# A fused two-layer transformer kernel: the first FFN's scales spread by the matrix engine, its weights issued later, all engine orders replaced

## The chip, the cores and the metric

The kernel runs on one NeuronCore of a Trainium2 chip. Its engines work side by side, each on its own queue: TensorE (PE, matrix products; PEld is its weight load), VectorE (DVE), ScalarE (ACT), GpSimd (POOL) and SyncE (SP), which here only issues DMAs. Results of PE land in PSUM, eight banks of 128 partitions by 512 fp32. The metric is the device time of one execution in microseconds; the median of three runs of the kernel before is 828.52 us (827.58 to 831.6).

## The reference

Sixteen sequences ("chunks", 0 to 15) of 256 tokens by 128 features go through two layers, each an attention and an FFN, with a residual sum and a layer norm after each of the four stages. All in fp32.

```python
x = layernorm(x + attn0(x))   # low-rank q, k; 16 heads of 8; causal
x = layernorm(x + ffn0(x))    # ternary weights with scales, below
x = layernorm(x + attn1(x))   # 16 heads of 8; not causal
x = layernorm(x + ffn1(x))    # top-1 expert: base weights plus a LoRA of rank 4

def tlin(x, w, s):            # w: 512x128, 512x512 or 128x512; s: one scale per output
    return jnp.einsum('bsi,oi->bso', x, w) * s
h = silu(tlin(x, w1, s1)) * tlin(x, w2, s2)
h = gelu(tlin(h, h1, hs1))
h = gelu(tlin(h, h2, hs2))
ffn0 = tlin(h, w3, s3)
```

## The kernel before

Each stage of a chunk is cut into steps, and one letter stands for each kind of step (table `KIND`). For every engine a string in `SEQUENCE` gives the order of its steps over all chunks and stages, and `walk` calls them in that order; `BANK_TABLE` says which PSUM bank each PE step writes. So the order is written out by hand, and an engine that waits for a semaphore holds up all that stands behind it. Stages of different chunks are interleaved: while chunk 5 is in its first FFN, chunk 6 is in its first attention, and so on.

The steps that matter here:

- `qk` projects queries and keys (PE, L955); ACT and DVE split them into two parts (L604/L608 and L719), SP writes them to a DRAM scratch ("parks" them, L471) and reads them back spread over the partitions ("fetches" qrow and krow, L480 and L484). `pass1` (PE, L988; the causal mask by L995) makes the scores from them, and DVE takes their row maxima (L745).
- `maxima` turns the maxima (PE, L1019); DVE splits them (L778, L780); SP writes them to `mrow` (L492). `pass2` makes the scores again (L1044), turned, and subtracts the maxima through `mrow` (L1052, L1059); ACT takes the exponential (L622), POOL masks (L565), `values` is the product with v (L1077), `project` the output product (L1089).
- Chunk 0 goes without scratch: its queries and keys lie in `hid` and in `prob`; `early` and `maxima` turn its maxima by L1005.
- The first FFN: `gated` (L1110), `hidden` (L1128, four steps of 8 products), `down` (L1185). Its ternary weights are multiplied by their scales once, at the start, on DVE: step `scale` with k = 0 (w12, L699 and L700), 1 and 2 (wh, 128x2048 each, L711), 3 (w3, L704).
- Step `late` is ACT issuing weight loads: k = 0 the scales, read from DRAM 128 times so that all partitions hold them, and w12; k = 1 both halves of wh (1 MB each) and w3; k = 2 the ten loads for layer 1.
- SP's `load` brings the next chunk's input, both ways round, once PE has used the buffer's last content.

## Time and profile before

| | us |
|---|---|
| median of 3 runs | 828.52 |
| the profiled execution | 828.5 |
| its span (first to last instruction) | 826.8 |
| PE busy | 792.4 |
| DVE busy | 619.0 |
| ACT busy | 412.1 |
| POOL busy | 186.3 |

1.7 us of the profiled execution lie around the span. PE is busy for 96% of it, so what counts is the time in which PE idles or runs at a lower clock, and the amount of work given to it. "PEclk" is the clock granted to PE as a share of full speed; a window at 0.50 is one at 1.2 instead of 2.4 GHz. A matmul record can be half of a product: L1128 has 8 products in a step and 16 records. "Idle before" is the time for which the engine stood still before a group, with the instruction whose end released it.

### The profile page before, as it was taken

The numbers are of one execution on the slowest core, as the hardware profiler recorded it, in microseconds if no ns is written. First come the engines' busy times: TensorE is split into PE (matmuls) and PEld (weight loads), VectorE is DVE, ScalarE is ACT, GpSimd is POOL, SyncE is SP. The second block draws the span as 40 slices with busy tenths as digits, with TensorE's granted clock in tenths as the row PEclk, the third lists the DMA queues.
The fourth block names the chain that finished last, engine by engine and source line by source line (L and its number), as shares of the span: only waits on it lengthen the run. The fifth ranks groups of instructions, "written<-read, shape, count | busy, mean of one in ns | idle before, by whom it ended". The sixth has DMA issues, their size and how long they took to land.

```text
span 826.8 us, 21566 instructions
## 1 busy us (share of the span) xinstructions
PE 792.4 (96%) x8626; PEld 610.8 (74%) x8626; DVE 619.0 (75%) x1749; ACT 412.1 (50%) x829; POOL 186.3 (23%) x397
## 2 busy tenths in 40 slices
PE   8879999999999999999999999999999999999796
PEld 6557777777778687887768777776878777786575
DVE  3666696886888697978779776788968776476775
ACT  1223517364744638374463646355393636636372
POOL 4221303031301313140222312130132303101022
PEclk9769999999999999999999999999999999999799
DMA  4652221304130314004050220304131110101200
GB/s 144 197 199 78 66 105 49 123 28 143 35 135 17 105 60 144 33 29 142 17 163 19 98 81 29 128 5 141 57 103 54 33 55 22 59 29 59 90 10 27
DMA packets 42572, 64.31 MB, mean 78 GB/s; under 512 B 5128, under 2 KB 33128, under 8 KB 42088
## 3 DMA queue, kind: packets, MB, share of 16 engines
q1 hardware_dynamic: 40696, 57.93, 21.5%
q10 hardware_dynamic: 1776, 5.00, 1.9%
q8 instruction: 69, 1.13, 0.6%
q14 instruction: 31, 0.25, 0.1%
HBM read 43.54 MB, written 18.35 MB: 75 GB/s over the span
## 4 chain that ended last, share of the span: by engine, by line
PE 79%; DMA 8%; DVE 5%; ACT 3%; SPq 2%; issue 2%; POOL 1%; POOLq 0%; DVEq 0%; ACTq 0%
PE banks L1128 26%; PE banks L1077 10%; PE banks L1044 6%; PE banks L988 6%; PE banks L1185 6%; PE banks L1110 6%; DMA krow<-scratch 5%; PE banks L955 3%; PE banks L1157 3%; DMA scratch<-split 2%; PE banks L1089 2%; PE banks L964 2%; ACT prob L622 2%; PE banks L1059 2%; PE banks L1052 2%
## 5 line engine op out<-in xcount | busy, mean ns | idle before, releaser
L745 DVE TENSOR_REDUCE top<-banks 128x3 f32<-128x384 f32 (+1 forms) x512 | 286.6, 613 | 50.5 <-PE banks L988 24.9
L622 ACT ACTIVATE prob<-banks 128x384 f32<-128x384 f32 (+1 forms) x512 | 242.5, 559 | 82.3 <-PE banks L1052 30.3
L636 ACT ACTIVATE hid<-banks 128x512 f32<-128x512 f32 x64 | 38.2, 597 | 211.8 <-PE banks L1128 211.6
L1077 PE MATMUL banks<-prob,v 128*32 128x256 f32 (+1 forms) x2048 | 117.9, 364 | 2.0 <-DVE low L875 1.2
L1128 PE MATMUL banks<-glu,wh 128*128 128x256 f32 x512 | 118.2, 384 | 0.1
L1128 PE MATMUL banks<-hid,wh 128*128 128x256 f32 x512 | 117.4, 382 | 0.2
L558 POOL TENSOR_TENSOR ln_rstd<-ln_var,minus_half 128x2 f32<-128x2 f32 x64 | 44.7, 702 | 320.7 <-DVE ln_var L824 320.4
L1128 PEld LDWEIGHTS banks<-glu,wh 128*128 128x128 f32 x512 | 94.8, 190 | 14.9 <-issue 1.1
L1128 PEld LDWEIGHTS banks<-hid,wh 128*128 128x128 f32 x512 | 94.8, 190 | 13.9 <-DVE top L745 1.2
L1077 PEld LDWEIGHTS banks<-prob,v 128*32 128x32 f32 x2048 | 58.9, 111 | 41.3 <-issue 10.0
L563 POOL TENSOR_TENSOR pool_carrier<-minus_half 128x1 f32<-128x1 f32 x128 | 25.3, 197 | 278.7 <-ACT prob L622 278.4
L988 PE MATMUL banks<-krow,qrow 32*128 32x256 f32 (+1 forms) x992 | 73.1, 337 | 10.7 <-DMA krow<-scratch 9.2
L565 POOL TENSOR_SCALAR_AFFINE_SELECT prob<-prob 128x512 f32<-128x512 f32 x128 | 83.2, 650 | 0.0
L988 PEld LDWEIGHTS banks<-krow,qrow 32*128 32x128 f32 x992 | 45.3, 189 | 44.9 <-issue 18.8
L1044 PE MATMUL banks<-qrow,krow 32*128 32x256 f32 x992 | 67.8, 325 | 1.4 <-issue 0.7
L1044 PEld LDWEIGHTS banks<-qrow,krow 32*128 32x128 f32 x992 | 43.6, 188 | 34.1 <-issue 21.3
L1110 PE MATMUL banks<-xt,w 128*128 128x256 f32 x256 | 63.9, 395 | 0.6 <-DVE top L745 0.5
L1110 PEld LDWEIGHTS banks<-xt,w 128*128 128x128 f32 x256 | 47.5, 194 | 9.4 <-issue 2.2
L786 DVE STREAM_TRANSPOSE osum<-banks 128x256 f32<-128x256 f32 x64 | 28.2, 442 | 31.8 <-PE banks L1077 31.7
L553 POOL TENSOR_TENSOR resid<-x,rows 128x256 f32<-128x256 f32 x48 | 35.2, 738 | 35.4 <-DVE ln_sum L811 35.3
L834 DVE TENSOR_SCALAR x<-ln_sum,ln_stat,ln_rstd 128x128 f32<-128x128 f32 x96 | 35.9, 418 | 8.6 <-POOL ln_rstd L558 8.6
L650 ACT ACTIVATE inter<-banks,cols 128x256 f32<-128x256 f32 x64 | 25.2, 488 | 25.9 <-PE banks L1165 25.8
(113 smaller groups left out, 1024.9 us busy)
## 6 DMA issues: line engine op xcount, KB each, us to landing
scratch<-split SPq DMA_DIRECT2D x124, 128.0 KB, 2.2
qrow<-scratch SPq DMA_DIRECT2D x31, 512.0 KB, 3.8
krow<-scratch SPq DMA_DIRECT2D x62, 256.0 KB, 4.3
xt<-in_xt SPq DMA_DIRECT2D x16, 128.0 KB, 2.2
wh<-in_wh ACTq DMA_DIRECT2D x2, 1024.0 KB, 6.3
out<-xout SPq DMA_DIRECT2D x16, 128.0 KB, 2.1
x<-in_x SPq DMA_DIRECT2D x15, 128.0 KB, 2.3
prob<-in_qk_a SPq DMA_DIRECT2D x2, 512.0 KB, 5.4
```

The costliest lines, as they stand in the source:

```text
L558: nc.gpsimd.tensor_tensor(ln_rstd[s][:], ln_var[s][:], minus_half[:], ALU.pow).then_inc(rstd[s], 1)
L565: nc.gpsimd.affine_select(out=diag, in_=diag, compare_op=ALU.is_ge, fill=0.0, base=0, pattern=[[0, 2], [0, QB], [1, P]], channel_multiplie ...
L622: nc.scalar.activation(prob[s][:, j % 2, g, 0:wide], banks[:, b, 0:wide], ACT.Exp, scale=1.0 / float(np.sqrt(np.float32(HD))) if s == A0 e ...
L636: nc.scalar.activation(hid[layer][:, 2 * m:2 * m + 2, :].rearrange("p m t -> p (m t)"), banks[:, g, :], ACT.Gelu).then_inc(gelued, 1)
L745: nc.vector.tensor_reduce(out=top[s][:, :, h], in_=banks[:, b, 0:blocks * wide].rearrange("p (q k) -> p q k", q=blocks), axis=AX, op=ALU.m ...
L834: done = nc.vector.tensor_scalar(x[into[s]][n % AHEAD][:, t, :], ln_sum[s][:, t, :], ln_stat[s][:, t, 0:1], ln_rstd[s][:, t:t + 1], ALU.su ...
L988: done = nc.tensor.matmul(banks[:, bs[g], start:start + wide], of_tile(queries, g, j, bass.ts(qb, P)), of_tile(keys, g, j, slice(0, wide)) ...
L1044: done = nc.tensor.matmul(banks[:, bs[g], kb * SEQ:(kb + 1) * SEQ - q0], of_tile(keys, g, j, bass.ts(kb, P)), of_tile(queries, g, j, slice ...
L1077: done = nc.tensor.matmul(banks[32 * i:32 * i + 32, g, q0:SEQ], v[s][:, kb, GROUP * j + i, :], prob[s][:, j % 2, i, kb * SEQ:(kb + 1) * SE ...
L1110: done = nc.tensor.matmul(banks[:, g, i * TOK:(i + 1) * TOK], w12[:, side, (2 * m + i) * P:(2 * m + i + 1) * P], xt[F0][n % AHEAD][:], sta ...
L1128: done = nc.tensor.matmul(banks[:, g, i * TOK:(i + 1) * TOK], wh[:, layer, k, (2 * m + i) * P:(2 * m + i + 1) * P], (glu, hid[0])[layer][: ...
L1185: done = nc.tensor.matmul(banks[:, g, t * D:(t + 1) * D], src[:, k, t * P:(t + 1) * P], w[:, k, :], start=k == 0, stop=k == HB - 1)
```

## The change

The scales are loaded into one partition (8 KB instead of 1 MB). PE multiplies a row of ones with them, one 512-wide fp32 product for each of the four sets, into PSUM, and DVE reads the scales for w12 and wh from there. So `scale` is now also a PE step (two products for k = 0, one each for k = 1 and 2) and takes banks. `late` has four parts instead of three: wh's first half, then wh's second half and w3, are issued separately. All five strings of `SEQUENCE` and the whole bank table are new; DVE's k = 0 to 2 no longer wait for the weights1 load. All other work is as before in kind and number.

```diff
-BARE = ('load', 'late', 'scale', 'keys', 'resid', 'fetch', 'norm', 'store', 'outputs')
+BARE = ('load', 'late', 'keys', 'resid', 'fetch', 'norm', 'store', 'outputs')
...
     "pe": (
-        "adcaaadeffgahfhaafahhgaicffajhfrfhdrahhscasgaisasftfjdfhuchayzrfrahhsigAsaAsaAsAftBfjarCrufhyChDadfDCsgC"
+        "adacaeavfgfadahhfafahchgaifvfvjhfrrdhfsasahhasgcaisaftjfdauryarhfhgfshAhAsAisaAsafBtfcjazChfuryCrfDCDCd"
...
     "act": (
-        "dxdffffffffffffxffffxfffffffjfffffrffffdrssssffffffjffdfffuyfrffffrssssfffffjfffrCCCCruffyffCCCCfffCdCfC"
+        "dxffffffffdffffffffxffffffffjxffffrrxfffdfssssfffjfffdfuryfrffffffffssssffffffffjCCCfCfufrfyCCrCCffffCCC"
...
-            "scale": [(k,) for k in range(4)],
-            "late": [(k,) for k in range(3)],
+            "scale": [(k,) for k in range(4 if engine == "dve" else 3)],
+            "late": [(k,) for k in range(4)],
...
-        scales = early[:, HEADS * D:HEADS * D + 4 * HID].rearrange("p (s o) -> p s o", s=4)
+        scales = early[0:1, HEADS * D:HEADS * D + 4 * HID].rearrange("p (s o) -> p s o", s=4)
...
-                    act.dma_start(early[:, HEADS * D:HEADS * D + 4 * HID], d_in["scales"].partition_broadcast(P)).then_inc(weights2, DMA)
+                    act.dma_start(early[0:1, HEADS * D:HEADS * D + 4 * HID], d_in["scales"].unsqueeze(0)).then_inc(weights2, DMA)
                     act.dma_start(w12[:], d_in["w12"]).then_inc(weights2, DMA)
                 elif k == 1:
-                    for layer, there in enumerate((weights3, weights4)):
-                        act.dma_start(wh[:, layer], d_in["wh"][:, layer]).then_inc(there, DMA)
+                    act.dma_start(wh[:, 0], d_in["wh"][:, 0]).then_inc(weights3, DMA)
+                elif k == 2:
+                    act.dma_start(wh[:, 1], d_in["wh"][:, 1]).then_inc(weights4, DMA)
                     act.dma_start(w3raw, d_in["w3"]).then_inc(weights4, DMA)
...
-            def scale(s, n, k):
-
+            def scale(s, n, k, *bs):
+
+                if k < 3:
+                    dve.wait_ge(scales_full, k + 2)
                 if k == 0:
-                    dve.wait_ge(weights1, NWEIGHTS1)
-                    dve.wait_ge(weights2, NWEIGHTS2)
-                    nc.vector.tensor_tensor(w12[:, 0, :], w12[:, 0, :], scales[:, 0, :], ALU.mult).then_inc(scaled_w, 1)
+                    nc.vector.tensor_tensor(w12[:, 0, :], w12[:, 0, :], banks[:, bs[0], :], ALU.mult).then_inc(scaled_w, 1)
...
+            def scale(s, n, k, *bs):
+
+                pe.wait_ge(weights2, NWEIGHTS2)
+                pe.wait_ge(ones_made, 1)
+                for i, g in enumerate(bs):
+                    at = 0 if k == 0 else k + 1
+                    last.wait(pe, g)
+                    nc.tensor.matmul(banks[:, g, :], ones[0:1, :].bitcast(F32), scales[:, at + i, :], start=True, stop=True).then_inc(scales_full, 1)
+                    last.used(g, scaled_w, at + i + 1)
```

Line numbers of the new kernel are higher by 3 for PE up to the turning steps (L988 is now L991, L1044 is L1047) and by 13 behind them (L1110 is now L1123).

PE, from chunk 0's last scores on, before: chunk 2's projection (L955) stands ahead of chunk 0's first turned maxima (L1005).

```order
L988 MATMUL banks<-prob,hid 128x128 x4
L988 MATMUL banks<-prob,hid 128x256 x4
L995 MATMUL banks<-block_ident,above 128x2x32 x16
L955 MATMUL banks<-xt_0,wq 128x256 x2
L1005 MATMUL banks<-ident,prob 128x128 x4
L1044 MATMUL banks<-hid,prob 128x256 x4
L1044 MATMUL banks<-hid,prob 128x128 x4
L1044 MATMUL banks<-hid,prob 128x256 x4
L1044 MATMUL banks<-hid,prob 128x128 x4
L1005 MATMUL banks<-ident,prob 128x128 x4
L988 MATMUL banks<-krow_1,qrow_1 128x128 x4
```

The same place in the new kernel (the rows start with chunk 0's first turned maxima):

```order
L1008 MATMUL banks<-ident,prob 128x128 x4
L991 MATMUL banks<-prob,hid 128x128 x4
L991 MATMUL banks<-prob,hid 128x256 x4
L998 MATMUL banks<-block_ident,above 128x2x32 x16
L1112 MATMUL banks<-prob,ones 128x512 x2
L1047 MATMUL banks<-hid,prob 128x256 x4
L1047 MATMUL banks<-hid,prob 128x128 x4
L1008 MATMUL banks<-ident,prob 128x128 x4
L1047 MATMUL banks<-hid,prob 128x256 x4
L1047 MATMUL banks<-hid,prob 128x128 x4
L991 MATMUL banks<-krow_1,qrow_1 128x128 x4
L991 MATMUL banks<-krow_1,qrow_1 128x256 x4
```

Chunk 2's projection has moved from before chunk 0's second scores to behind chunk 1's first scores (two rows below the last shown), the turned maxima are one step earlier, and the two scale products (L1112) have come in ahead of chunk 0's second scores.

ACT, the weight loads, before (`inter<-in_w` is w3):

```order
L587 DMA prob<-in_scales 128x2048
L588 DMA w<-in_w 128x1024
L604 ACTIVATE split<-banks 128x512
L622 ACTIVATE prob<-banks 128x384 x12
L591 DMA wh<-in_wh 128x2048 x2
L592 DMA inter<-in_w 128x512
L622 ACTIVATE prob<-banks 128x384 x4
L597 DMA wq<-in_qk_w 128x256
L597 DMA wv<-in_v_w 128x128
```

ACT in the new kernel, from wh's first half on:

```order
L591 DMA wh<-in_wh 128x2048
L624 ACTIVATE prob<-banks 128x384 x8
L629 ACTIVATE xt_0<-banks 128x256
L593 DMA wh<-in_wh 128x2048
L594 DMA inter<-in_w 128x512
L624 ACTIVATE prob<-banks 128x384 x4
L633 ACTIVATE glu<-banks 128x512 x2
L599 DMA wq<-in_qk_w 128x256
L599 DMA wv<-in_v_w 128x128
```

wh's halves are now eight exponentials and a transpose copy apart; the ten loads of layer 1 (the two rows from L599 on are their first) stand behind both tanh steps of the first FFN (L633) and, among others, ahead of chunk 3's split.

PE at the last chunk, from its second-layer projection (L955, wq of layer 1) to its first scores (`krow_1`), before:

```order
L955 MATMUL banks<-xt_1,wq 128x256 x2
L1098 MATMUL banks<-ident,x_0 128x128 x2
L988 MATMUL banks<-krow_0,qrow_0 128x256 x8
L1077 MATMUL banks<-prob,v 32x256 x16
L1019 MATMUL banks<-ident,top 128x128 x2
L1139 MATMUL banks<-wgl,xt_0 128x40 x2
L964 MATMUL banks<-wv,xt_0 128x128 x2
L1089 MATMUL banks<-wo,yt_1 128x128 x2
L1157 MATMUL banks<-xt_1,wi 128x256 x4
L1165 MATMUL banks<-lowt,wlb 128x256 x4
L1148 MATMUL banks<-ident,low 128x128 x2
L988 MATMUL banks<-krow_1,qrow_1 128x256 x8
```

The same projection in the new kernel:

```order
L958 MATMUL banks<-xt_1,wq 128x256 x2
L1080 MATMUL banks<-prob,v 32x256 x8
L1047 MATMUL banks<-qrow_1,krow_1 128x256 x8
L1055 MATMUL banks<-mrow_1,ones 128x512 x4
L1080 MATMUL banks<-prob,v 32x256 x8
L991 MATMUL banks<-krow_0,qrow_0 128x256 x8
L1047 MATMUL banks<-qrow_1,krow_1 128x256 x8
L1055 MATMUL banks<-mrow_1,ones 128x512 x4
L1080 MATMUL banks<-prob,v 32x256 x8
L991 MATMUL banks<-krow_0,qrow_0 128x256 x8
L1161 MATMUL banks<-ident,low 128x128 x2
L1198 MATMUL banks<-wout,inter 128x128 x8
```

Behind these rows come half of a values step (L1080 x8), the turned maxima (L1022) and then the last chunk's first scores (L991 on `krow_1`): thirteen rows of other work now lie between projection and scores, where ten lay before. At the last chunk's own maxima (L1019, now L1022) the order before had the second FFN's first product (L1157 and L1165), v, routing and 16 value products ahead of the second scores; now there are a transpose, routing, v and the same 16 value products.

## Rows read from the trace of the kernel before

**Rows 1.** The page, part 1: busy time, share of the span and instructions of each engine

```profile
PE 792.4 (96%) x8626; PEld 610.8 (74%) x8626; DVE 619.0 (75%) x1749; ACT 412.1 (50%) x829; POOL 186.3 (23%) x397
```

**Rows 2.** Windows: PE, PEld, DVE, ACT, POOL busy (count), PEclk, share of DMA, GB/s

```profile
0.00:90.00 90.00, 77.33 (x853) 59.08 (x854) 54.22 (x132) 23.50 (x48) 25.63 (x66) 0.85 0.45 145
90.00:760.00 670.00, 661.27 (x7277) 512.04 (x7277) 518.50 (x1453) 359.76 (x718) 150.91 (x317) 1.00 0.22 73
760.00:826.80 66.80, 53.80 (x502) 39.70 (x502) 46.32 (x165) 28.88 (x65) 9.76 (x14) 0.89 0.13 40
16.90:45.30 28.40, 24.07 (x332) 17.10 (x335) 20.49 (x48) 7.75 (x18) 6.31 (x16) 0.79 0.66 220
26.30:36.60 10.30, 9.52 (x84) 6.45 (x83) 5.53 (x12) 3.88 (x9) 3.21 (x8) 0.50 0.53 169
50.30:63.90 13.60, 12.68 (x129) 9.93 (x130) 8.88 (x23) 5.90 (x14) 6.20 (x14) 0.50 0.23 56
```

**Rows 3.** Timeline of PE to 75 us: start, duration, group, idle time before it

```profile
26.04 1.77 PE L955 MATMUL banks<-xt,wq 128*128 128x256 f32 x4 [2.85 <-DMA x<-in_x]
...
50.84 0.80 PE L988 MATMUL banks<-krow,qrow 32*128 32x128 f32 x8 [4.07 <-DMA krow<-scratch]
...
70.52 3.72 PE L1128 MATMUL banks<-glu,wh 128*128 128x256 f32 x16
```

**Rows 4.** Chain of waits, end of the span: start, duration, what

```profile
762.54 0.85 ACT split L608 x2
...
767.53 0.56 SPq L480
...
773.28 0.51 PE banks L988 x7
...
784.93 0.44 PE banks L988 x8
785.37 1.98 PE banks L1185 x16
...
788.25 0.37 PE banks L1019 x2
...
790.82 0.45 PE banks L964 x4
...
798.70 0.44 PE banks L1044 x8
799.14 0.24 PE banks L1052 x3
799.38 1.00 PE banks L1077 x16
```

**Rows 5.** Timeline of SP's queue: chunk 1 parked, chunk 1 and chunk 2 fetched

```profile
19.21 2.94 SPq L471 DMA_DIRECT2D scratch<-split  x4
27.36 0.57 SPq L480 DMA_DIRECT2D qrow<-scratch  x1
...
42.06 0.56 SPq L480 DMA_DIRECT2D qrow<-scratch  x1
```

**Rows 6.** Windows: while the wide weights landed, and one within, PE alone

```profile
38.00:50.80 12.80, 8.39 (x134) 5.20 (x126) 8.79 (x20) 3.05 (x8) 3.09 (x8) 0.85 0.94 325
...
43.00:44.00 1.00, 1.00 (x32) 0.73 1.11 459
```

**Rows 7.** Timeline of ACT's DMA queue: w12, then layer 1's first and last load

```profile
18.29 0.45 ACTq L588 DMA_DIRECT2D w<-in_w  x1
...
42.19 0.36 ACTq L597 DMA_DIRECT2D wq<-in_qk_w  x1
...
47.77 0.45 ACTq L597 DMA_DIRECT2D wout<-in_wo  x1
```

**Rows 8.** Timeline of PE: second attention's maxima turned, then its second scores

```profile
127.39 0.38 PE L1019 MATMUL banks<-ident,top 128*128 128x128 f32 x2
...
131.93 0.51 PE L1044 MATMUL banks<-qrow,krow 32*128 32x256 f32 x8
```

More of the change, by code:

```diff
@@ L121 @@
+        "nnnnQJnnRmoKwnKnnnJnnRnnQnKonnnwmQJnRnQnnRmnnnnwonJnnnmQKnnwnRKnnJonnnmoRKwQnnnJnnnQnnmnnwnnnRnJnonKmnnw"
+        "nnQnKnonnmwJRQRKJwRQKJJRKQJQRRQQ"
     ),
     "sp": (
[L123 to L124 removed]
+        "ppdpqdqgpdqgpdyLqgBpyLdqgBpyLgdqpByLdqgBpyLdgSqBpyLdqgpByLdqgBpySLdqgBSpyLgSdqBpyLgdqBypLSpdSgqBdqySLgBy"
+        "SLgByLSyBLSSyLBSBSSSS"
     ),
@@ L146 @@
+    "57026135470261354760213754607524165204763521047263517042617310542361705243651274635120743561247351024673"
+    "52014673201674351607423547163205471643205764351263054127564031264107342610527615276143527603145036124750"
+    "36130562731405627304156427306514207635174026357012463570214674032167540327165342701653742016742301674354"
+    "701625347016534702651347025613472516"
 )
@@ L185, in shared_banks @@
         elif step[0] not in BARE:
-            count = {"gated": 2, "expert": 2, "pass1": GROUP, "pass2": GROUP}.get(step[0], 1)
+            count = {"gated": 2, "expert": 2, "pass1": GROUP, "pass2": GROUP, "scale": 2 - (step[-1] > 0)}.get(step[0], 1)
             of[step] = [int(b) for b in BANK_TABLE[bank:bank + count]]
@@ L692, in _ @@
             last = Last()
-            def scale(s, n, k):
+            def scale(s, n, k, *bs):
+                if k < 3:
+                    dve.wait_ge(scales_full, k + 2)
                 if k == 0:
-                    dve.wait_ge(weights1, NWEIGHTS1)
-                    dve.wait_ge(weights2, NWEIGHTS2)
-                    nc.vector.tensor_tensor(w12[:, 0, :], w12[:, 0, :], scales[:, 0, :], ALU.mult).then_inc(scaled_w, 1)
-                    nc.vector.scalar_tensor_tensor(out=w12[:, 1, :], in0=w12[:, 1, :], scalar=0.5, in1=scales[:, 1, :],
+                    nc.vector.tensor_tensor(w12[:, 0, :], w12[:, 0, :], banks[:, bs[0], :], ALU.mult).then_inc(scaled_w, 1)
+                    nc.vector.scalar_tensor_tensor(out=w12[:, 1, :], in0=w12[:, 1, :], scalar=0.5, in1=banks[:, bs[1], :],
                                                    op0=ALU.mult, op1=ALU.mult).then_inc(scaled_w, 1)
                 elif k == 3:
+                    dve.wait_ge(weights1, NWEIGHTS1)
                     dve.wait_ge(weights4, 2 * DMA)
@@ L710, in scale @@
                         dve.wait_ge(weights4, 2 * DMA)
-                    nc.vector.tensor_tensor(wh[:, k - 1], wh[:, k - 1], scales[:, 1 + k, :].unsqueeze(1).to_broadcast([P, HB, HID]),
+                    nc.vector.tensor_tensor(wh[:, k - 1], wh[:, k - 1], banks[:, bs[0], :].unsqueeze(1).to_broadcast([P, HB, HID]),
                                             ALU.mult).then_inc(scaled_w, 1)
@@ L1188, in down @@
                 last.used(g, ln[s], 5 * n + 1)
-            walk(dict(warm=warm, qk=qk, v=v_, pass1=pass1, maxima=maxima, early=early, pass2=pass2, values=values, project=project, turn=turn, gated=gate, hidden=hidden, route=route,
+            walk(dict(warm=warm, scale=scale, qk=qk, v=v_, pass1=pass1, maxima=maxima, early=early, pass2=pass2, values=values, project=project, turn=turn, gated=gate, hidden=hidden, route=route,
                       lora=lora, expert=expert, down=down), "pe")
```

78 lines of the change are left out of this document (36 added, 42 removed).

## The prediction

> **What bounds the kernel now.** I read the busy times first: PE works for 792.4 of 826.8 us and no other engine for more than 75% [rows 1]. The windows then say where the other 34.4 us lie: between 90 and 760 us PE is busy for 661.3 of 670.0 us at full clock; in the first 90 us it is idle for 12.7 us and has a mean clock of 0.85; in the last 66.8 us it is idle for 13.0 us at 0.89 [rows 2]. At half clock a microsecond does half a microsecond's work, so the clock costs up to 0.15 x 90 = 13.5 us at the start and 0.11 x 66.8 = 7.3 us at the end. The middle has little to give. An order can win at the ends, or lose in the middle.
>
> The timeline of PE shows what the start waits for. At 26.04 it has waited 2.85 us for chunk 2's input; at 50.84 it has waited 4.07 us for chunk 2's fetched rows [rows 3]. After the first wait it ran at half clock for 10.3 us, after the second for 13.6 us [rows 2]. Both transfers were late because the DMA engines were full: they were 94% busy from 38.0 to 50.8 us at 325 GB/s [rows 6]. In that stretch lay wh (2 MB), w3, the ten loads of layer 1 and chunk 2's fetch, which was issued at 42.06 [rows 5].
>
> **The change part by part.**
>
> *Start, up to chunk 2's first scores.* The broadcast of the scales (1 MB) is gone, and chunk 1 is parked before chunk 2's input is asked for. Chunk 2's projection no longer stands on PE ahead of chunk 0's second scores, so the 2.85 us wait goes. What paces PE next is DVE. From 16.9 us to the end of chunk 1's maxima at 45.3 DVE works for 20.5 of 28.4 us [rows 2], and the new order gives it the same pieces in that stretch: 32 maxima, two splits, two shifts, w12's scaling, one v. The gaps, 7.9 us, came from the wait for chunk 2's input, from PE at half clock and from the late start of chunk 1. Chunk 1's fetch was issued at 27.36 though its parking began at 19.21 [rows 5]; without the broadcast I put it at about 24, before DVE has finished chunk 0. I leave 2.6 us of gaps, a third of the old ones, for the handing to and fro between PE and DVE around chunk 0's shifts: 16.9 + 20.5 + 2.6 = 40.0 instead of 45.3.
>
> Chunk 2's first scores need its fetch, and that waits for PE's last second scores of chunk 0 (two buffers). In the new order those stand two short steps before the end of chunk 1's scores, so at about 38.5. From issue to use a fetch took 773.28 - 767.53 = 5.75 us where little else moved [rows 4]. wh's first half is issued behind chunk 0's last exponentials, some 2 us after the fetch; 1 MB at 325 GB/s [rows 6] is 3.2 us, of which I charge a third: 38.5 + 5.75 + 1.1 = 45.35. Before it was 50.84: **-5.5 us**. Bounds: 43.5 (fetch a little earlier, alone on the DMA engines), 48 (PE at half clock as from 26.3 to 36.6, whole sharing), so -7.3 to -2.8. PE still waits here, some 4 us as before, and I keep the half clock behind it.
>
> *Four scale products.* No product like them is in the trace. L1128 makes eight 256-column fp32 products (16 records) in 3.72 us, so one is 0.47 us and 512 columns are 0.93 us at full clock [rows 3], 1.86 at half. The lower bound is the 0.24 us in which L1052 sends its 512-column products over two rows each [rows 4], in another number format; nothing excludes that one row is cheap. The row nearest in format is L1128, so I take 0.93. The first two stand where PE waits for DVE anyway; if that cover is gone they cost up to 1.9 us. The other two stand among chunk 1's second scores, in the stretch at half clock, with nothing beside them that PE could do: 2 x 1.86 = **+3.7 us** (+0.5 to +3.7). In exchange v of chunk 1 (0.45 us at full clock [rows 4], 0.9 at half) has moved ahead of the wait: **-0.9 us**. DVE reads the scales from PSUM for 512 or 2048 elements as it did from SBUF; the order between wh's scaling and the hidden layers leaves several microseconds, so 0 (-0.5 to +0.5).
>
> *Layer 1's ten loads on ACT.* Their issue held ACT's queue from 42.19 to 48.22 us [rows 7], while ACT had nothing to do. Now they stand behind both tanh steps and ahead of chunk 1's last exponentials and chunk 3's split: 6.0 us of delay for these. PE has behind them a projection (0.9), values (1.0), one second-scores step (0.7), two hidden steps of 3.7, two first scores and two values, about 13 us before it needs the exponentials: covered. Chunk 3's fetch comes 6 us later and has some 19 us of PE work until use; needed are 10.7 (762.54 to 773.28 [rows 4]) plus 6 plus 1.7 for the exponentials: covered with little to spare. **+0.5 us** (0 to +3).
>
> *End.* The last chunk's scores can't start before 10.7 us after its projection [rows 4]. Work between, from the order with durations of [rows 4]: before, three transposing steps 1.1, first scores 0.4, values 2.0, v and output product 0.9, routing 0.4, an expert step 2.3 (an estimate: four products of 0.47 and the LoRA part) = 7.1. After: four half values steps 4.0, two second scores (0.44 + 0.24) 1.4, two first scores 0.9, a transpose 0.3, down 1.98, turned maxima 0.4 = 9.0. So 1.9 us less standing still, and the half clock that follows the wait (most of the 7.3 us) should shrink; between 0 and 6 us I take 2.1, since a wait of 1.7 us remains. Against this: at the last chunk only about 3.2 us of work lie between its turned maxima and its second scores. The shortest gap in the trace that shows no wait there is 131.93 - 127.77 = 4.16 us [rows 8]; +0.8. Together **-3.2 us** (-7 to +1).
>
> *Middle.* Counting the order in the same way, the second attention's gap between turned maxima and second scores is 4.2 us of work or less at seven chunks, where before it was so at two. By the 4.16 us above this costs about 0.1 to 1.1 us each, and the projections of chunks 3, 8 and 13 have more cover than before. **+0.9 us** (-3 to +5).
>
> Sum: -5.5 + 3.7 - 0.9 + 0.5 - 3.2 + 0.9 = -4.5 us on the profiled execution of 828.5 us (span 826.8 and 1.7 around it), so 824.0. The median of the three runs, 828.52, is the same number.
>
> **The clock, once more.** From 43.0 to 44.0 PE was busy all the time and yet the mean granted clock was 0.73, so it fell to the lower level (1.2 GHz) without a long pause ahead [rows 6]. The Trainium skill, "TensorE: Matmul & The Clock Gate", section "A second HAM failure mode: psum-queue depth-cycling", says that short idle moments between groups of products, while banks are being freed, are enough to let the clock swing. This row agrees. By that rule the new start, in which PE is fed by DVE from 20 to 40 us, would fall to half clock as the old one did; this is the first rival.
>
> **The rivals.**
>
> *A: the start gains little.* The clock falls around 26 us with no long wait, because PE works in bits. At half clock for 10.3 us PE loses up to 5.1 us, of which the 2 us or so that DVE lags are hidden: chunk 2's first scores at 48, lead 2.8 instead of 5.5. With the end at -2 the sum is -2.8 + 3.7 - 0.9 + 0.5 - 2.0 + 0.9 = -0.6: 828. For it: the row of 43 us. Against: before, the fall at 26.3 came only after a wait of 2.85 us.
>
> *B: the clock stays up.* The fetch comes in 5 us and PE, itself later than I think, hardly waits; the 13.6 us at half clock [rows 2] shrink to a few, which gives up to 6.8 us and halves the price of the scale products (-1.9). -4.5 - 5 - 1.9 + 1 = -10.4: 818. For it: the fetch leads wh by some 2 us. Against: 5.75 us is what a quiet fetch takes, and PE has only a few steps to fill it.
>
> *C: slower, by the row maxima of the second attention.* The chain turned maxima, DVE's two splits, two issues on SP, landing, then L1055 has to fit behind less work at 11 of 16 chunks (5.0 us or less). If it takes 5.5 us, as it would when SP's queue holds a fetch or DVE is at first maxima, PE stands still for some 1.2 us at each, 13 us, and the start's gain doesn't pay: -4.5 - 0.9 + 13 = +7.6: 836. The change decides for slower from a chain of about 5 us on. Against: no wait on mrow is among the idle time of PE before.
>
> *D: no effect of the parts.* The waits move to the next late thing and the sum stays within 0.5% with neither end gaining: 828; counted with A.
>
> **How the numbers follow.** Forecast, 819.5 to 826: 0.40. A and D: 0.27. B: 0.18. C and other losses in the middle: 0.15. A measurement of this kernel tells 0.5% (4.1 us) from no change, so faster means below 824.4. Of the forecast 0.29 lies there and 0.11 above; with B that makes 0.47 faster, 0.37 the same (0.11, A and D less 0.01), 0.16 slower. The range for 8 in 10 takes in B and A and stops inside C: 814 to 832.
>
> **What would show it.** Right: in the new profile PE reaches chunk 2's first scores (L991 on krow_0) near 45 us with a wait for krow of about 4 us, DVE is busy over 85% from 17 to 40 us, the first hidden step (L1141) starts near 67 instead of 70.5 us, L1112 takes 0.9 us a product at full clock, PE's idle time from 760 us to the end is 10 to 12 us. Wrong: idle time before L1047 or L1055 between 90 and 760 us, mean clock below 0.85 in the first 90 us, a wait of PE for ACT near 65 to 75 us, or chunk 3's first scores waiting for its fetch.

## The result, and the profile after

The changed kernel takes 834.97 us (median of 20 executions, 827.24 to 844.18) beside 829.09 us of the kernel before (20 executions, 825.56 to 832.53). The ratio is 1.0052, with a 95% interval of 1.0032 to 1.0072: slower by half a percent, where 824.0 was forecast. A second set gave 832.96 against 828.50, ratio 1.0046 [1.0016, 1.0077]. An execution more than 1.5% above the fastest of its kernel (the 844.18 here, four more in the experiments) counts as slow and is left out of ratios and means.

Executions of one kernel differ by some 10 us, and at least half of that spread goes with the clock granted to PE. Every run lists its span and its mean granted clock; their product says how long the span would be at full clock. I call it the **clock-free time** below (a rough measure, since idle time under a lowered clock is discounted too; over the executions it has a standard deviation of 2.0 us, the span one of 2.4 in the kernel before and 4.1 in the changed one). It is 803.9 us for the kernel before (mean over 123 executions), 810.2 +- 0.5 (standard error) for the changed one, and 809.8 +- 0.7 in the second set. The clock took 22.5 us from the kernel before and 21.9 from the changed one. So the loss is work and waiting, +6.3 us, and not the clock: the profiled execution of the changed kernel, 830.4 us with a span of 828.6, was one of its luckier ones.

The windows of the changed kernel that answer to [rows 2] (windows: PE, PEld, DVE, ACT, POOL busy with counts, PEclk, DMA share, GB/s):

```profile
0.00:90.00 90.00, 81.96 (x891) 63.48 (x892) 56.26 (x139) 26.43 (x55) 25.30 (x67) 0.85 0.41 134
90.00:760.00 670.00, 655.86 (x7182) 510.06 (x7182) 513.12 (x1437) 348.62 (x702) 150.14 (x317) 0.99 0.22 73
760.00:828.60 68.60, 57.33 (x564) 40.40 (x562) 51.51 (x174) 31.97 (x71) 9.76 (x14) 0.96 0.11 35
```

PE idles for 8.0 us in the first 90 us instead of 12.7, at the same clock of 0.85. At the end it idles for 11.3 instead of 13.0 us, at 0.96 instead of 0.89. Both ends got better. The middle, from 90 to 760 us, got worse: 14.1 us idle instead of 8.7, and 6.8 us at half clock instead of none. In the profile of the second set it is 12.2 us idle and 20.5 us at half clock.

The timeline of PE, for [rows 3] (start, duration, group, idle time before it):

```profile
46.01 0.80 PE L991 MATMUL banks<-krow,qrow 32*128 32x128 f32 x8 [3.00 <-DMA krow<-scratch]
...
49.05 1.16 PE L1112 MATMUL banks<-prob,ones 1*128 1x512 f32 x1
...
51.61 2.01 PE L1112 MATMUL banks<-prob,ones 1*128 1x512 f32 x2
...
65.32 0.92 PE L1141 MATMUL banks<-glu,wh 128*128 128x256 f32 x3
```

Chunk 2's first scores start at 46.01, not 50.84; forecast was 45.35. The first hidden step starts at 65.32, not 70.52. In this profile the start did what the prediction said; not all kernels with this start did (below). L1112 is the scale products. Each has two records, which here stand among those of L1047: the first runs from 49.05 to 51.07 us (1.16 and then 1.06), the second is the x2 row, so both take 2.0 us at half clock.

The waits of PE between 90 and 760 us, first of the kernel before, then of the changed one (who waited for whom: total us, times, longest):

```profile
PE banks L988 <- DMA krow<-scratch: 2.9, 4, 1.0
```

```profile
PE banks L991 <- DMA krow<-scratch: 7.2, 8, 2.0
```

The largest new wait is for fetched rows of queries and keys, 4.3 of the 5.4 us (in the second profile 5.9 us in place of 7.2). And at one place the clock falls where it did not before (windows of the changed kernel, then of the kernel before):

```profile
168.00:170.00 2.00, 1.60 (x24) 1.09 (x22) 1.85 (x10) 1.81 (x5) 1.57 (x5) 1.00 0.02 4
170.00:172.00 2.00, 1.67 (x34) 1.39 (x34) 1.10 (x7) 2.00 (x6) 1.34 (x3) 0.87 0.43 122
172.00:178.00 6.00, 6.00 (x78) 3.54 (x70) 4.55 (x12) 1.28 (x4) 2.21 (x5) 0.50 0.02 6
```

```profile
168.00:170.00 2.00, 2.00 (x18) 1.80 (x17) 1.97 (x6) 1.85 (x3) 0.00 (x0) 1.00 0.04 8
170.00:172.00 2.00, 1.74 (x34) 1.37 (x36) 1.85 (x10) 1.90 (x6) 1.56 (x4) 1.00 0.00 0
172.00:178.00 6.00, 6.00 (x109) 4.39 (x104) 5.48 (x12) 3.02 (x9) 3.21 (x8) 1.00 0.17 52
```

PE idles for 0.73 us between 168 and 172, in three pieces (0.40, 0.16 and 0.17 us) while ACT works through twelve exponentials in a row, and then runs at half clock for 6 us, which costs 3. To see when the lead was lost I gave every kind of PE step one price (the scale products none) and compared when the two kernels had done equal work. The changed kernel leads by 2.8 us at 90 us and by 1.8 at 161; it trails by 2.1 at 182 and by 4.1 at 735; it ends 2.3 behind. In the profile of the second set the numbers are 3.3 ahead, 0.9 behind, 4.3 behind at 182, 8.2 and 8.0 behind; there most of the first loss lies between 90 and 110 us, with a wait of 1.75 us for krow at 108 us and falls of the clock at 92 and 109 us.

### The profile page after: what moved, and what is told of

It is laid out like the page before. It is cut to its first block and busy times, and to the rows that moved or that the text cites. A ratio compares the mean times of both kernels' runs of the same rounds, so it can differ in the third digit from the quotient of the medians.

```text
span 828.6 us, 21583 instructions
## 1 busy us (share of the span) xinstructions
PE 795.1 (96%) x8634; PEld 613.9 (74%) x8634; DVE 620.9 (75%) x1749; ACT 407.0 (49%) x825; POOL 185.2 (22%) x397
## 5 line engine op out<-in xcount | busy, mean ns | idle before, releaser
L1080 PE MATMUL banks<-prob,v 128*32 128x256 f32 (+1 forms) x2048 | 119.2, 365 | 1.4 <-DVE top L748 0.5
L1141 PEld LDWEIGHTS banks<-hid,wh 128*128 128x128 f32 x512 | 95.1, 191 | 14.1 <-DVE top L748 2.0
L1080 PEld LDWEIGHTS banks<-prob,v 128*32 128x32 f32 x2048 | 58.5, 111 | 42.7 <-issue 12.6
L991 PE MATMUL banks<-krow,qrow 32*128 32x256 f32 (+1 forms) x992 | 72.4, 338 | 13.0 <-DMA krow<-scratch 11.2
L991 PEld LDWEIGHTS banks<-krow,qrow 32*128 32x128 f32 x992 | 44.6, 188 | 46.7 <-issue 19.4
L1047 PE MATMUL banks<-qrow,krow 32*128 32x256 f32 x992 | 67.5, 323 | 1.1 <-ACT prob L624 0.4
L1047 PEld LDWEIGHTS banks<-qrow,krow 32*128 32x128 f32 x992 | 43.9, 186 | 32.0 <-issue 20.2
L1123 PE MATMUL banks<-xt,w 128*128 128x256 f32 x256 | 64.4, 399 | 0.2 <-DVE glu L848 0.2
L1123 PEld LDWEIGHTS banks<-xt,w 128*128 128x128 f32 x256 | 48.4, 198 | 9.2 <-issue 1.6
L837 DVE TENSOR_SCALAR x<-ln_sum,ln_stat,ln_rstd 128x128 f32<-128x128 f32 x96 | 36.7, 425 | 8.5 <-POOL ln_rstd L559 8.4
```

The source lines that it names most:

```text
L837: done = nc.vector.tensor_scalar(x[into[s]][n % AHEAD][:, t, :], ln_sum[s][:, t, :], ln_stat[s][:, t, 0:1], ln_rstd[s][:, t:t + 1], ALU.su ...
L991: done = nc.tensor.matmul(banks[:, bs[g], start:start + wide], of_tile(queries, g, j, bass.ts(qb, P)), of_tile(keys, g, j, slice(0, wide)) ...
L1047: done = nc.tensor.matmul(banks[:, bs[g], kb * SEQ:(kb + 1) * SEQ - q0], of_tile(keys, g, j, bass.ts(kb, P)), of_tile(queries, g, j, slice ...
L1080: done = nc.tensor.matmul(banks[32 * i:32 * i + 32, g, q0:SEQ], v[s][:, kb, GROUP * j + i, :], prob[s][:, j % 2, i, kb * SEQ:(kb + 1) * SE ...
L1123: done = nc.tensor.matmul(banks[:, g, i * TOK:(i + 1) * TOK], w12[:, side, (2 * m + i) * P:(2 * m + i + 1) * P], xt[F0][n % AHEAD][:], sta ...
L1141: done = nc.tensor.matmul(banks[:, g, i * TOK:(i + 1) * TOK], wh[:, layer, k, (2 * m + i) * P:(2 * m + i + 1) * P], (glu, hid[0])[layer][: ...
```

## The experiments

Each kernel is compared with executions of the kernel before in the same set. "CF" is the clock-free time; "idle" is PE's idle time between 90 and 760 us in the profile, 8.7 us in the kernel before and 14.1 in the changed one. Except where it is said, the orders of an experiment are pieces of the two, joined where PE's step of the number given ends.

| kernel | front | rest | scales | median | ratio, interval | CF | idle |
|---|---|---|---|---|---|---|---|
| changed, 2nd set | new | new | new | 832.96 | 1.0046 [1.0016, 1.0077] | 809.8 | 12.2 |
| order_alone | new | new | old | 841.42 | 1.0146 [1.0101, 1.0191] | 813.5 | 15.5 |
| new_start | new, 56 | old | new | 831.73 | 1.0034 [1.0005, 1.0063] | 805.7 | 8.9 |
| new_to_117 | new, 117 | old | new | 831.47 | 1.0028 [1.0006, 1.0051] | 806.4 | 9.6 |
| new_to_153 | new, 153 | old | new | 841.23 | 1.0129 [1.0085, 1.0173] | 811.4 | 15.2 |
| both_ends | new, 117 | old, new from 664 | new | 835.29 | 1.0071 [1.0044, 1.0098] | 811.5 | 13.1 |
| new_rest_b | old, 54 | new | old | 839.68 | 1.0109 [1.0067, 1.0150] | 809.1 | 17.4 |
| doubled | new | new | products twice | 835.93 | 1.0096 [1.0066, 1.0127] | 810.4 | 11.2 |
| filled | new | new | two moved | 832.68 | 1.0061 [1.0036, 1.0087] | 809.3 | 13.8 |
| no_products | new | new | none | 836.52 | 1.0103 [1.0061, 1.0144] | 812.9 | 16.8 |
| later_scores | new, 7 moves | new | new | 847.42 | 1.0226 [1.0178, 1.0273] | 819.0 | 16.6 |
| light_only | old | old | load only | 824.99 | 0.9954 [0.9933, 0.9975] | 803.4 | 9.0 |
| old_products | old | old | new, exposed | 833.85 | 1.0065 [1.0040, 1.0090] | 806.8 | 8.2 |
| slot | old | old | new, in the wait | 827.96 | 1.0000 [0.9978, 1.0021] | 805.8 | 9.2 |
| spread | old | old | new, three waits | 828.74 | 1.0009 [0.9984, 1.0034] | 804.0 | 8.9 |

CF has a standard error of 0.3 to 1.1 us. Each kernel ran 6 to 12 times. The sets ran on different chips, and the kernel before has medians of 827.46 to 829.49 in them (CF 803.1 to 804.6), so kernels of different sets are compared by their ratios.

### The changed kernel again, the orders alone, the new start alone

The second of these has the new strings and banks (without the products' part), but loads the scales into all partitions as before and has no products:

```diff
-act.dma_start(early[0:1, ...], d_in["scales"].unsqueeze(0)).then_inc(weights2, DMA)
+act.dma_start(early[:, ...], d_in["scales"].partition_broadcast(P)).then_inc(weights2, DMA)
-nc.tensor.matmul(banks[:, g, :], ones[0:1, :].bitcast(F32), scales[:, at + i, :], start=True, stop=True)
```

The third takes the first 56 PE steps of the new order, with what the other engines do for them, and the old order behind.

> The changed kernel once more, unedited, for a second profile and runs on the same chip as the others. All theories: 833 to 837 us, 0.4 to 0.8% above the kernel before. Theory M (the middle of the new order, 90 to 760 us, waits more often for the fetched rows, and the clock falls behind some of these waits): more idle time of PE and more microseconds at half clock between 90 and 760 us than the 8.7 us and none of before. Theory P (the scale products and their place are what eats the start's gain, the rest is scatter): idle time in the middle near 14 us as in the first profile, no more, and the first 90 us slower than there.

> The new orders with the scales as before: 1 MB broadcast by DMA, DVE reading them from SBUF, the four scale products of PE left out (a bank table without them), loads of wh in two steps as in the change. Theory P: the 3.7 to 4.4 us of the products come back, 1 to 2 us are lost to the later parking of chunk 1: 831 to 832 us. Theory M: the middle's loss stays and the start is little changed either way: 833 to 836 us, same as the changed kernel within 2 us.

> The new kernel's first 56 steps of PE (to about 90 us, all scale products and all weight loads within) with what belongs to them on the other engines, then all that is left in the order of the kernel before. Theory M: the start's gain stands alone, in the first profile 2 to 3 us at equal work: 826 to 827 us, faster than before by 0.3%. Theory P: the start is what loses: 832 to 835 us.

Measured: 832.96, 841.42 and 831.73. Neither theory has the last two. The new orders are 8 us slower still without the new way of the scales (3.7 in CF). The new start with the old rest isn't faster than the kernel before, but its middle is as tight as the old one (windows of new_start):

```profile
0.00:90.00 90.00, 78.96 (x860) 59.45 (x861) 53.93 (x130) 23.46 (x48) 25.20 (x66) 0.85 0.41 134
90.00:760.00 670.00, 661.15 (x7260) 511.89 (x7260) 517.43 (x1452) 358.62 (x715) 150.79 (x317) 1.00 0.22 73
```

661.15 us busy against 661.27 in [rows 2]. By equal work it has no lead at 90 us (0.2 behind), and it loses 2.6 us more at the seam, where PE waits for exponentials that the new start has left further behind (timeline of PE):

```profile
94.32 1.86 PE L958 MATMUL banks<-xt,wq 128*128 128x256 f32 x4 [2.00 <-ACT prob L624]
```

### Where the lead is lost

> PE's first 117 steps of the changed order (to 155 us, with what the other engines do for them), then the order before. Measured against equal matmul work, the changed kernel leads the kernel before by 1.8 us at 161 us and trails it by 1.9 from 177 us on, a stretch in which its clock falls. Theory M (the start's gain is real and the new middle loses it): the lead of 1 to 2 us at 160 us stays flat to the end, median 826 to 828, no clock fall at 170 to 180 us. Theory E (the start's lead is only work put off, so any seam shows it): the lead is gone within 30 us of the seam, as it is in the kernel with the new start of 56 steps, median 830 to 832.

> As the kernel with 117 steps, but with the changed order for 153 steps, to about 195 us, so past the stretch at 168 to 178 us. Theory M: the clock falls at 171 us as in the changed kernel, the curve steps by 3 to 4 us there and is flat behind it, median 3 to 4 us above the kernel with 117 steps (829 to 832). Theory E: the two end within 1 us of each other.

> The changed order for the first 117 steps and for those from 664 on (the last 90 us), the order before between them. Theory M: the end gives another 2 to 4 us as it does in the changed kernel's curve (trailing by 4.2 at 735 us, by 0 to 2 at the end), median 822 to 825, faster than both kernels. Theory E, or if the new end needs the new middle ahead of it: 829 to 833.

> The kernel before with its scales broadcast over the partitions and its first 54 steps as they were (to 93 us); the changed order from there. Theory M: the rest by itself loses 4 to 7 us by 735 us, gives 2 to 4 back in the end, median 831 to 835. Theory E: the rest by itself loses nothing, 827 to 829.

Measured: 831.47, 841.23, 835.29, 839.68; the last three lie above all that was forecast for them. The first theory got its place right and its price wrong. With the old rest from step 117 on there is no fall of the clock at 170 to 180 us, and from 110 to 750 us the curve of equal work moves by some 2 us. With the old rest from step 153 on the clock falls at 160 and at 176 us and again at 200, and the kernel is 10 us slower. Not all of that is the price of these 36 steps: by equal work it falls behind new_to_117 by 4.1 us up to 182 us, and most of the rest is lost at its seam, where PE waits longest (timeline of PE):

```profile
203.68 0.69 PE L1101 MATMUL banks<-ident,x 128*128 128x128 f32 x2 [4.60 <-DVE x L837]
```

new_to_117 was forecast at 826 to 828 and took 831.5, the number of the second theory. In its profile chunk 2's first scores start at 48.7 us, 2.7 later than in the changed kernel, though every engine's instructions are the same up to there. In new_start and new_to_153 they start at 48.7 too, in both_ends at 47.7, in the second profile of the changed kernel at 45.7. Half clock set in at 26.3 us for 10 us in these three (in both_ends at 24.6 for 10), and at 23.7 to 24.7 us for 7 us in the changed kernel. By equal work these four lead by -0.2 to 1.6 us at 90 us, the two profiles of the changed kernel by 2.8 and 3.3. Chunk 2's fetch is issued at 37.7 and 38.1 us in these two, and at 40.2 to 40.7 in the three. So the start's gain goes with the length of this first half clock. Why it is 10 us here and 7 there with equal instructions, the profiles don't say.

The end: both_ends trails from a new seam of its own, where PE waits 2.9 us for row maxima (waits of PE, 730 to 760 us):

```profile
PE banks L1101 <- DVE top L748: 2.9, 1, 2.9
```

So it says nothing on the worth of the new end. The last one says most: the new rest behind the old front has twice the idle time of the old rest. (Joined three PE steps later, the old front and the new rest wait for each other in a circle, so that kernel has no time.)

```profile
90.00:760.00 670.00, 652.56 (x7153) 506.88 (x7154) 510.02 (x1424) 344.66 (x695) 149.59 (x316) 0.99 0.22 71
```

Across all kernels with the old rest whole the idle time is 8.2 to 9.6 us; in those with the new rest it is 11.2 to 17.4. (new_to_153, with 15.2, and both_ends, with 13.1, stand between: 4.6 and 2.9 us of theirs are the waits at their seams.)

### The price of the products

Doubled:

```diff
+nc.tensor.matmul(banks[:, g, :], ones[0:1, :].bitcast(F32), scales[:, at + i, :], start=True, stop=True)
 nc.tensor.matmul(banks[:, g, :], ones[0:1, :].bitcast(F32), scales[:, at + i, :], start=True, stop=True).then_inc(scales_full, 1)
```

Filled moves the products for the hidden layers from behind chunk 2's first scores to ahead of them, and ACT copies them out of PSUM, `nc.scalar.activation(scales[:, 2 + i, :], banks[:, g, :], ACT.Identity)`. In old_products all four stand ahead of chunk 2's projection, PE's step 6:

```diff
-act.dma_start(early[:, ...], d_in["scales"].partition_broadcast(P)).then_inc(weights2, DMA)
+act.dma_start(early[0:1, ...], d_in["scales"].unsqueeze(0)).then_inc(scales_in, DMA)
+for i, g in enumerate(bs):      # PE, four products
+    nc.tensor.matmul(banks[:, g, :], ones[0:1, :].bitcast(F32), scales[0:1, i, :], start=True, stop=True).then_inc(scales_full, 1)
+for i, g in enumerate(bs):      # ACT, four copies
+    nc.scalar.activation(scales[:, i, :], banks[:, g, :], ACT.Identity).then_inc(scales_kept, 1)
```

> The changed kernel with each of the four scale products issued twice into its bank; nothing else differs. If the products cost what the prediction put (3.7 us for the four, the first two largely beside a wait), four more at the same places cost 3 to 5 us at equal clock: span times clock rises from 810.0 to 813 to 815, median 836 to 839. If they are hidden by the waits around them: within 1 us of the changed kernel. If a stretch at half clock makes them dear: 6 us or more.

> The changed kernel with the products of the two hidden layers moved ahead of chunk 2's first scores, into PE's wait of 3.0 us at 43 us; ACT, idle there, copies the two banks to SBUF for DVE. If the two products cost what their rows say where they stand now (1.16 and 2.01 us at half clock, with what waits behind): 2 to 3 us less than the changed kernel, median 830 to 832. If the place doesn't matter, because what follows waits for something else: 833 to 835.

> All five orders of the kernel before, with the one part of the change that cuts traffic: the 8 KB load in place of the 1 MB broadcast, and four products on PE, put ahead of chunk 2's projection, where PE waits 2.85 us for x; ACT copies the banks to SBUF. If the lighter traffic is where the start's gain comes from and the new orders are where it is lost: x and the first krow land 2 to 5 us sooner, PE's wait of 4.07 us at 46.8 us shrinks, the rest runs as before, median 824 to 827, faster than both kernels. If the gain needs the new order of the start: 828 to 831.

Measured: 835.93, 832.68, 833.85. Filled can't be told from the changed kernel (CF 809.3 +- 0.6 against 810.2 +- 0.5): the place of these two doesn't show in the new orders. Old_products is slower than both of its theories. In the old orders the exposed products are dear. Timeline of PE in old_products:

```profile
26.34 6.27 PE L1203 MATMUL banks<-prob,ones 1*128 1x512 f32 x8 [0.45 <-DVE top L753]
32.54 2.08 PE L963 MATMUL banks<-xt,wq 128*128 128x256 f32 x4
```

The wait of 2.85 us for x is gone [rows 3], and 6.27 us of products stand in its place, most of them at half clock. In the new orders four more products cost nothing that can be told in CF: 810.4 against 810.2. The times say otherwise, with less certainty: ratios of 1.0096 [1.0066, 1.0127] with eight and 1.0052 [1.0032, 1.0072] with four products are 3.6 us apart, which CF puts down to the clock (it took 23.5 us here and 21.9 there). So the first theory has the median and the second the CF. They did cost 3.0 us at 90 us by the curve of equal work; by 600 us these had come back, from the waits:

```profile
PE banks L991 <- DMA krow<-scratch: 4.3, 6, 1.2
```

That is the doubled kernel between 90 and 760 us; the changed one waits 7.2.

### Traffic alone, products left out, scores put off

> The kernel before with its orders and the 8 KB load in place of the 1 MB broadcast, and no products: DVE multiplies by a row of constants that is there anyway, so the weights of the first FFN carry other factors than the scales. It prices the lighter traffic alone. If that is worth what the prediction gave the start (5.5 us together with the orders): x and krow land sooner, 822 to 826. If PE waits for something else as soon as the traffic is gone, as the kernel with the old orders and exposed products suggests (806.8 of span times clock, of which four products in a row at half clock are 3.1 to 3.4 at full speed, against 803.9 before): within 1 us of before.

> The changed kernel without the four products, DVE multiplying by a row of constants, so the first FFN's weights carry other factors than the scales. If the products cost 3.7 us, as predicted: span times clock falls from 810.0 to 806.3, median 829 to 831. If they cost as little as four more of them did in the doubled kernel (0.2 us): 809.5 to 810.5, median 833 to 835.

> The changed kernel with the first scores of seven chunks (second attention 0, 1, 6, 7, 10, first attention 12 and 14) moved behind the one or two PE steps that follow them, where PE waited for krow (6.9 us in all in the profile of the changed kernel). If those waits are what the new middle costs: the wait for krow between 90 and 760 us falls from 7.2 to under 3 us, span times clock by 3 to 5 us, median 829 to 831. If a wait only moves to the next step that needs the chunk, or what is behind waits for DVE instead: less than 1 us.

```diff
-nc.vector.tensor_tensor(w12[:, 0, :], w12[:, 0, :], scales[:, 0, :], ALU.mult)
+nc.vector.tensor_tensor(w12[:, 0, :], w12[:, 0, :], rows[:, 0:HID], ALU.mult)
```

(light_only and no_products, for w12 and both halves of wh; in no_products DVE's first scaling also waits for the weights1 load again. later_scores only changes the string of PE and leaves DVE's order as it was.)

Measured: 824.99, 836.52, 847.42. The load alone makes the kernel before faster, 0.9954 [0.9933, 0.9975]. That is what the change's idea is worth before anything is paid for it. In CF it is 0.9 us (803.4 against 804.4 of the kernel before in the same set, which is within the noise) and the clock takes 19.6 us instead of 22.4: in the first 90 us the profile has 20.5 us at half clock, that of the kernel before 27.3. PE then waits longest here (timeline of light_only):

```profile
46.60 0.80 PE L988 MATMUL banks<-krow,qrow 32*128 32x128 f32 x8 [5.72 <-DMA krow<-scratch]
```

4.2 us earlier than in [rows 3], and with a longer wait. The changed kernel without its products isn't faster but 2.7 us slower in CF, and waits more for krow:

```profile
PE banks L991 <- DMA krow<-scratch: 10.1, 9, 1.6
```

Both of its theories had 829 to 835. With none, four and eight products this wait is 10.1, 7.2 and 4.3 us between 90 and 760 us: in these three profiles, the less PE does at the start, the longer it stands still later. That speaks against PE's work as what bounds the new orders. In later_scores the wait for krow is down to 0.6 us, and more waits for DVE have taken its place (PE, 90 to 760 us):

```profile
PE banks L991 <- DVE top L748: 4.5, 8, 0.8
PE banks L1101 <- DVE x L837: 1.9, 2, 1.3
PE banks L1047 <- DVE top L748: 1.5, 2, 0.8
```

with CF at 819.0, 9 us more. The row of L837 is there in the changed kernel too; the waits for row maxima in all rose from 1.8 to 9.3 us. DVE's order was left as it was, so DVE too stands still for the scores that come later, and its maxima come in later than what stands behind them expects. The run shows that moving PE's steps alone makes it worse. It doesn't show what the new orders would take without the waits for krow. The two theories for this run named both outcomes; both stayed under a loss of 1 us.

### Four products, three places

In slot the four products stand ahead of chunk 2's first scores in the old orders, DVE's scaling of w12 behind them. In spread one stands ahead of the first second-scores, one ahead of chunk 1's first scores, two where slot has four.

```diff
 SEQUENCE["pe"], step 22:  ... maxima(chunk 1)  +scale x4  pass1(chunk 2) ...
 SEQUENCE["act"], step 21: ... late(k=2)  +scale x4  pass2(chunk 1) ...
```

> The orders of the kernel before with the 8 KB load, and the four products (the true scales, at full precision) in one place: ahead of chunk 2's first scores, where PE waits 5.72 us for krow, DVE 4.71 us and ACT longer in the kernel with the load alone (824.99 us). ACT copies the four banks to SBUF; DVE's scaling of w12 moves behind them. Products take 0.85 us each at full clock and 1.7 at half, so 3.4 to 6.8 us against a wait of 5.7. If the wait hides them: within 1 us of the kernel with the load alone, 824 to 826, faster than the kernel before and than the changed one. If the clock, kept from idling, falls earlier, or the first scores are put off: 827 to 829. In front of chunk 2's projection the same products cost 9 us (833.85).

> As the kernel with all four products in the wait for krow (827.96 us), but one product ahead of the first second-scores, where PE waits 0.78 us for DVE at full clock, one ahead of chunk 1's first scores, where it waits 0.75 to 1.79 us for krow at full clock, and two in the long wait. Two at half clock are 3.4 us against 5.7, so all four should be hidden. If the place and the clock there decide a product's price: 824 to 826, faster than the kernel before and than the changed one. If each still puts off the chain of the start: 827 to 829.

Measured: 827.96 and 828.74, the second theory both times, and both no different from the kernel before (1.0000 [0.9978, 1.0021] and 1.0009 [0.9984, 1.0034]) and better than the changed one. Neither keeps the 4 us of the lighter traffic. The products in slot (timeline of PE):

```profile
43.33 5.49 PE L1203 MATMUL banks<-prob,ones 1*128 1x512 f32 x6
...
48.61 1.06 PE L1203 MATMUL banks<-prob,ones 1*128 1x512 f32 x1
...
49.46 1.06 PE L1203 MATMUL banks<-prob,ones 1*128 1x512 f32 x1
```

They are busy from 43.3 to 50.5 us. ACT copies their four banks at 45.43, 47.14, 48.85 and 50.55, so one product takes 1.71 us at half clock, four 6.8 us, and the wait to be filled was 5.7. By the curve of equal work light_only leads the kernel before by 4.5 us at 90 us, slot by 0.6. No kernel that computes the right result beat the kernel before.

## Why the prediction was wrong, point by point

- **Start, -5.5 us, v moved, -0.9.** Right in the two profiles of the changed kernel. Chunk 2's first scores came at 46.01 (forecast 45.35) after a wait of 3.00 (some 4), the first hidden step at 65.32 (67). DVE was busy for 18.6 of the 23.1 us from 16.9 to 40, 81% and not 85%. The lead of 2.8 us at 90 us (3.3 in the second) is the forecast's -5.5 + 3.7 - 0.9 = -2.7. That it came out so closely is in part luck: with equal instructions up to there, four other kernels led by -0.2 to 1.6 us, and in three of them chunk 2's first scores came at 48.7 us behind 10 us at half clock. That is rival A's case, which had them at 48.
- **Four scale products, +3.7 us.** The size of a product was right: 1.71 us at half clock where I had 1.86, and 2.0 us as the rows show in place. (The expectation of filled took 1.16 us, half of a product, for a whole one.) Its effect on the end is open: neither doubling the four nor leaving them out moves the changed kernel's clock-free time by their cost (812.9, 810.2, 810.4 with none, four, eight), though by the ratios doubling them costs 3.6 us. In the old orders they cost some 4 to 9 us (ratios of 0.9954 without them, and of 1.0000, 1.0009 and 1.0065 with them in three places).
- **Ten loads on ACT, +0.5.** Chunk 3's split came 5.0 us after its projection, against 6.0 forecast, and PE waited neither for it nor for ACT from 65 to 75 us: covered.
- **End, -3.2.** In the right direction: 11.3 us idle (forecast 10 to 12) and a clock of 0.96 (0.92 in the second profile). The last chunk's wait for krow fell from 1.74 to 0.91 us, where 1.9 us less was forecast, and the +0.8 for its maxima wasn't due: its second scores came 3.57 us behind the turned maxima without a wait. By equal work the changed kernel regains 1.8 us from 735 us on, in the second profile 0.2. Smaller than forecast, and the profiled execution was lucky in its clock.
- **Middle, +0.9.** This step failed. By equal work the changed kernel loses 6.9 us from 90 to 735 us in the first profile and 11.5 in the second, beyond my bound of +5. I had counted the gaps between turned maxima and second scores, and looked at the projections of chunks 3, 8 and 13 alone. At those gaps no wait on mrow appeared, down to 3.56 us (chunk 8), shorter than my 4.16: rival C's mechanism isn't there, and that its 836 lies near the measured time is luck. What is there are waits for krow, 7.2 us instead of 2.9. Five of the eight stand in the second attention, with 10.2 to 11.5 us of work between a projection and its scores, where the rows landed 10.9 to 13.2 us after the projection; stretches as short stood in the order before too. The other three have 15 to 21 us of work: there the parking itself was issued 11.1, 9.2 and 4.9 us after the projection (first attention of chunks 12 and 14, second attention of chunk 13), where the order before had 0.7, 0.7 and 1.2. So there the orders of the other engines made the chain late, which a count of PE's work can't see (rows below). And there are short waits for ACT's exponentials, behind which the clock fell at 171 us. It fell there, between 171 and 177 us, in six of the nine profiles of kernels with the new order in that place (not in doubled, filled and later_scores), and in none of the eight with the old order there. The same three idle pieces, 0.72 to 0.74 us, are in all nine. And doubled, which has no half clock in its middle at all, has the same CF as the changed kernel, so these falls alone aren't what the 6.3 us are.

The late parking of chunk 12 in the changed kernel (timelines of PE and of SP's queue; the first parking is that of another chunk, the last row chunk 12's), then in the kernel before:

```profile
462.16 1.06 PE L958 MATMUL banks<-xt,wq 128*128 128x256 f32 x4
...
466.46 2.52 SPq L472 DMA_DIRECT2D scratch<-split  x4
470.53 0.57 SPq L481 DMA_DIRECT2D qrow<-scratch  x1
471.14 1.25 SPq L485 DMA_DIRECT2D krow<-scratch  x2
472.49 1.22 SPq L493 DMA_DIRECT2D mrow<-tsplit  x2
473.76 0.44 SPq L498 DMA_DIRECT2D out<-xout  x1
474.30 3.00 SPq L472 DMA_DIRECT2D scratch<-split  x4
```

```profile
456.55 1.13 PE L955 MATMUL banks<-xt,wq 128*128 128x256 f32 x4
...
458.38 3.52 SPq L471 DMA_DIRECT2D scratch<-split  x4
```

- **Rival A**, that the start gains little since the clock falls anyway, had the first half right, and the second in the kernels named above. The clock fell at about 25 us, with PE idle for 0.65 us of the 5 us before, in one wait for DVE (windows of the changed kernel):

```profile
20.00:25.00 5.00, 4.35 (x65) 3.17 (x59) 4.97 (x16) 0.00 (x0) 0.00 (x0) 0.97 0.79 226
25.00:30.00 5.00, 5.00 (x52) 4.25 (x52) 3.05 (x7) 1.92 (x5) 1.55 (x4) 0.50 0.56 199
```

The Trainium skill, "TensorE: Matmul & The Clock Gate", section "A second HAM failure mode: psum-queue depth-cycling", says that short idle moments between groups of products can make the clock swing; the prediction weighed it. The trace agrees at 170 us in kind (three short pieces, behind ACT's exponentials), and less at 25 us, where it was a single wait. The three profiles with the same pieces and no fall show that such moments don't decide it alone.

The mistake behind the failed step: I took "the middle has little to give" for "the middle has little to lose". I checked the new order for one chain, for the other at three chunks alone, and for both by PE's work alone. A sentence of the prediction said that an order can lose in the middle, and its sum then gave this 0.9 us.

Not settled: how much of the 6.3 us the waits for krow are, and what else bounds the new rest. No run shortened the chain from projection to fetched rows (by an earlier split or parking) or moved DVE's maxima together with PE's scores, and no run made DVE's work less. Nor is it known why equal instructions reach chunk 2's first scores at 46 us in two profiles and at 48.7 in three.

## What to carry to other kernels

When all orders are replaced, most of the risk lies in the long tight stretch and not at the ends: for every chain that was just covered there (here park and fetch, exponentials, row maxima), compare the work between its start and its use in the old and the new order. A wait seen on one engine isn't a price that can be taken away by moving one step; take it away in one run, with the other engines' orders moved along, before believing it. A kernel pieced together from two orders can lose more at the join (2.0, 2.9 and 4.6 us in single waits here) than the piece under test is worth, so look at the join first. And work put into an engine's wait is free only for as long as it lasts at the clock that holds there: four products of 0.85 us at full clock fitted a wait of 5.7 us on paper and took 6.8 at half clock.

## What the runs showed of the hardware

- A wait of 0.73 us in all, in pieces within 4 us, was followed by 6 us at 1.2 GHz (168 to 178 us), while the kernel before, idle for 0.26 us there, kept 2.4 GHz. The same pieces stand in nine profiles; in six the clock fell behind them, in three it didn't.
- With an 8 KB load in place of the 1 MB broadcast near 18 us, chunk 2's first scores came 4.2 us earlier, 46.60 instead of 50.84. PE no longer waits for the x of [rows 3], and chunk 1's fetch is issued at 23.77 us instead of 27.36 [rows 5].
- A product of one row by 512 columns in fp32 took 1.71 us at 1.2 GHz (slot: ACT's copies of four in a row start 1.71 us apart).
- With equal instructions and equal banks up to there, chunk 2's first scores came at 45.7 and 46.0 us in two profiles and at 48.7 in three; the first stretch of half clock, from about 25 us on, had lasted 6.8 us in the two and 10.2 in the three.
